# A two-stage adapter kernel: generator and first down-projections one step later, tile 1 in its own PSUM banks, other orders at both ends

## The reference

```python
scale = cond @ norm_w.T + 1.0                                   # [32, 256]
h = x * (scale[:, None, :] * rsqrt(mean(x * x) + 1e-6))
val, gate = split(h @ up_w.T, 2)                                # 1024 each
h = val * gelu(gate)
hq = round(h * 127 / max|h| per row) * max|h| / 127             # to 8 bits
wq = clip(round(down_w / mean|down_w|), -1, 1) * mean|down_w|   # ternary
x1 = hq @ wq.T + x

Wd_b = Wd + 0.1 * (cond @ Wdd.T + bdd)       # one 128 x 256 matrix for each sequence
Wu_b = Wu + 0.1 * (cond @ Wdu.T + bdu)       # one 256 x 128 matrix for each sequence
out = x1 + relu(x1 @ Wd_b.T + bd) @ Wu_b.T + bu
```

## Time and profile before

| | |
|---|---|
| median of 3 runs | 480.67 us (480.03 to 480.86) |
| the profiled execution | 480.89 us, its span 479.2 us |
| PE busy | 467.1 us, 97% |
| DVE, ACT, POOL busy | 377.8 (79%), 365.5 (76%), 260.2 us (54%) |
| mean granted TensorE clock | 0.995 of full speed |
| HBM read, written | 37.44 MB, 8.39 MB |

### The profile page before, as it was taken

The page is one execution under the profiler, slowest core; times in us unless marked ns, Lnnn a source line. Parts: engine busy times, 40 slices in busy tenths (PEclk is TensorE's granted clock), DMA queues, the critical chain, the costliest instruction groups (busy, mean ns, idle before and its releaser), DMA issues.

```text
span 479.2 us, 10039 instructions
## 1 busy us (share of the span) xinstructions
PE 467.1 (97%) x3278; PEld 271.3 (57%) x3278; DVE 377.8 (79%) x789; ACT 365.5 (76%) x636; POOL 260.2 (54%) x676
## 2 busy tenths in 40 slices
PE   8989999999999999999999999999999999999995
PEld 7445656666565455555555555555555555555563
DVE  4798988898898787877877788786777877777776
ACT  5889999999997678768676876867776777777662
POOL 0295775657655446475573746557374543444653
PEclk9999999999999999999999999999999999999997
DMA  7957787777873455565554466455445544544332
GB/s 269 349 113 205 180 244 227 189 210 181 253 176 89 92 121 100 137 147 117 148 133 107 128 141 155 111 153 126 103 136 133 143 103 119 130 123 90 72 85 89
DMA packets 117860, 71.01 MB, mean 148 GB/s; under 512 B 102000, under 2 KB 102960, under 8 KB 115632
## 3 DMA queue, kind: packets, MB, share of 16 engines
q1 hardware_dynamic: 117648, 70.29, 57.2%
q10 hardware_dynamic: 160, 0.07, 0.1%
HBM read 37.44 MB, written 8.39 MB: 96 GB/s over the span
## 4 chain that ended last, share of the span: by engine, by line
PE 88%; DVE 5%; ACT 3%; issue 2%; DMA 1%; POOL 0%; DVEq 0%; ACTq 0%; SPq 0%; POOLq 0%
PE bank L1022 64%; PE bank L1036 11%; PE bank L1113 4%; PE bank L1127 4%; PE bank L1095 4%; PE bank L993 1%; DVE adapt L716 1%; ACT gel L552 1%; DVE xs_lo L746 1%; DMA qT<-qn 1%; DVE hid L767 1%; DVE amax L775 1%; ACT tern L650 0%; ACT qn L574 0%; DVE x L879 0%
## 5 line engine op out<-in xcount | busy, mean ns | idle before, releaser
L767 DVE SCALAR_TENSOR_TENSOR hid<-bank,rms,gel 128x512 f32<-128x512 f32 x127 | 95.2, 750 | 80.4 <-ACT gel L552 79.4
L552 ACT ACTIVATE gel<-bank,rms 128x512 f32<-128x512 f32 x127 | 86.9, 684 | 90.7 <-PE bank L1022 90.6
L1022 PE MATMUL bank<-up_hi,xs_hi 128*128 128x512 f16 x508 | 151.2, 379 | 3.0 <-DVE hid L767 1.5
L1022 PE MATMUL bank<-up_lo,xs_hi 128*128 128x512 f16 x508 | 151.1, 379 | 0.7 <-DVE up_lo L931 0.7
L1022 PE MATMUL bank<-up_hi,xs_lo 128*128 128x512 f16 x508 | 151.1, 379 | 0.0
L1022 PEld LDWEIGHTS bank<-up_lo,xs_hi 128*128 128x128 f16 x508 | 49.6, 98 | 60.9 <-DVE up_lo L931 1.4
L1022 PEld LDWEIGHTS bank<-up_hi,xs_lo 128*128 128x128 f16 x508 | 49.7, 98 | 59.9
L775 DVE TENSOR_REDUCE amax<-hid 128x1 f32<-128x1024 f32 x63 | 76.9, 1220 | 2.2
L565 ACT ACTIVATE hid<-hid,amax 128x1024 f32<-128x1024 f32 x64 | 72.4, 1132 | 2.3 <-DVE amax L781 1.8
L403 POOL TENSOR_TENSOR wsplit<-stage,wsplit 128x288 f16<-128x288 f32 x64 | 52.8, 853 | 34.9 <-ACT wsplit L527 34.9
L1022 PEld LDWEIGHTS bank<-up_hi,xs_hi 128*128 128x128 f16 x508 | 48.3, 98 | 38.5 <-DVE xs_lo L746 2.9
(11 more groups left out here) (129 smaller groups left out, 633.3 us busy)
## 6 DMA issues: line engine op xcount, KB each, us to landing
xT_s<-in_xT SPq DMA_DIRECT2D x32, 256.0 KB, 3.0
xn_s<-in_xn SPq DMA_DIRECT2D x32, 256.0 KB, 3.1
stage<-in_WddT SPq DMA_DIRECT2D x8, 1024.0 KB, 5.4
stage<-in_WduT SPq DMA_DIRECT2D x8, 1024.0 KB, 5.2
out<-out_s SPq DMA_DIRECT2D x31, 256.0 KB, 2.4
adapt<-in_up_wT SPq DMA_DIRECT2D x4, 512.0 KB, 6.8
x<-in_down_wT SPq DMA_DIRECT2D x1, 1024.0 KB, 10.0
qT<-qn SPq DMA_TRANSPOSE x63, 3.1
```

Source lines behind the costliest of these rows:

```text
L552: nc.scalar.activation(gel[:, c], u_gate[c][:], ACT.Gelu, scale=rms[:, t // TPB % XN_SLOTS, t % TPB:t % TPB + 1]).then_inc(gelu_done, 1)
L767: nc.vector.scalar_tensor_tensor(out=hid[:, t % 2, c * 512:(c + 1) * 512], in0=u_val[c][:], scalar=rms[:, t // TPB % XN_SLOTS, t % TPB:t % ...
L1022: ins = nc.tensor.matmul(dst[:], a[:, t // TPB % 2, k, cols], w[:, c, k, v, :], start=(k == 0 and n == 0), stop=(k == KD - 1 and n == 2))
```

## The change

Generator chunks move one step later (`chunk`), and with them the adapter (`adapter_step`). The root of sequence 2 is at step 3. Down-projections 0 and 1 are both in step 4, and down(2) in step 5 as before; residual(0) is in step 4, residual(1) and (2) in step 5. Tile 1's up-projection goes to banks 5, 6, 7 and 4 and waits for nobody. The absolute sum is made in two halves, as the down weights come in two, and PE adds the two in bank 5 in step 2; ternary_first moves from step 1 to step 2, ternary_second ahead of, and ternary_third behind, quant_scale(2). The first root and the squares of sequences 0 and 1 go behind the up weights' conversion, xn of sequences 0 and 1 behind the up weights in the queue, base and bias ahead of sequence 2 and chunk 0. Two `idle` matmuls go. In the tail q_transpose goes ahead of down(62), middle(30) ahead of the last transposes, output_bias(30) ahead of middle_low(29), total(28) and residual_high(61) ahead of the evacuation of the transposed tile.

```diff
-N_SMALL = 6
+N_BASE = 4
+N_SMALL = 2
-IDLE_SECOND = 9
+IDLE_SECOND = 7
...
 def adapter_step(b):
-    return max(2 * b + 7, NGEN + 5 + (4 * b + 2) // 3)
+    return max(2 * b + 7, NGEN + 6 + (4 * b + 2) // 3)
 def scales(s):
-    return [b for b in range(1, B) if max(2 * b - 2, 1) == s]
+    return [b for b in range(2, B) if max(2 * b - 2, 3) == s]
+def downs(s, c):
+    late = {(4, 0): [0], (4, 1): [1]}
+    return late.get((s, c), [s - DOWN] if c == 0 and s - DOWN >= 2 else [])
+def residuals(s):
+    return {4: [0], 5: [1, 2]}.get(s, [s - DOWN] if s - DOWN > 2 else [])
 def chunk(s, lag):
-    return [s - 2 - lag] if 0 <= s - 2 - lag < NGEN else []
+    return [s - 3 - lag] if 0 <= s - 3 - lag < NGEN else []
...
-        sum_ps = y_ps[:, 0:1]
+        sum_ps = bank[5][:, 0:1]
+        second_val = [bank[5], bank[7]]
+        second_gate = [bank[6], bank[4]]
+        def u_banks(t, c):
+            return (second_val[c], second_gate[c]) if t == 1 else (u_val[c], u_gate[c])
...
@@ SP, before the loop
-            load_x(0)
+            sp.dma_start(xT_s[:, 0], xT[0]).then_inc(ld_xT[0], 16)
             for n in range(NC * KD):
                 sp.dma_start(raw_up[:, n // KD, n % KD], up_wT[:, n // KD, n % KD]).then_inc(ld_up[n], 16)
-            load_x(1)
-            sp.dma_start(raw_down, down_wT).then_inc(ld_down, 16)
+            for b in range(2):
+                sp.dma_start(xn_s[:, b], xn[b]).then_inc(ld_xn[b], 16)
+            for i in range(2):
+                part = slice(i * JF * D // 2, (i + 1) * JF * D // 2)
+                sp.dma_start(raw_down[:, part], down_wT[:, part]).then_inc(ld_down[i], 16)
+                if i == 0:
+                    sp.dma_start(xT_s[:, 1], xT[1]).then_inc(ld_xT[1], 16)
+            for i, (w, b) in enumerate(((WdT, bddT), (WuT, bduT))):
+                sp.dma_start(base[:, i, :], w).then_inc(ld_base, 16)
+                sp.dma_start(bias_raw[:, i, :], b).then_inc(ld_base, 16)
+            load_x(2)
             load_chunk(0)
-            load_x(2)
...
@@ POOL
             def base_sum():
-                pool.wait_ge(ld_small, 16 * N_SMALL)
+                pool.wait_ge(ld_base, 16 * N_BASE)
...
             residual_low(LAST_T - 2)
+            output_bias(B - 2)
             middle_low(B - 3)
-            output_bias(B - 2)
+            pool.wait_ge(x1_lo_done, LAST_T - 2)
+            output_bias_last(1)
             middle_low(B - 2)
-            output_bias_last()
+            output_bias_last(0)
@@ ACT
+            def absolute_sum(i):
+                part = slice(i * JF * D // 2, (i + 1) * JF * D // 2)
+                act.wait_ge(ld_down[i], 16)
+                nc.scalar.activation(tern[:].rearrange("p j d -> p (j d)")[:, part], raw_down[:, part], ACT.Abs,
+                                     accum_out=wsum[:, 3 * i:3 * i + 1]).then_inc(absum_ready, 1)
             scaled_high(0)
-            squares(0)
             (the four up_hi)
+            squares(0)
+            squares(1)
+            absolute_sum(0)
             for s in range(NT):
...
                 gelu(s, 0)
                 if s == 0:
+                    gelu(0, 1)
                     scaled_high(1)
-                    squares(1)
-                    gelu(0, 1)
-                    (the absolute sum)
+                if s == 1:
+                    absolute_sum(1)
+                    gelu(1, 1)
...
             quantized(LAST_T)
+            residual_high(LAST_T - 2)
             qT_evacuate()
-            residual_high(LAST_T - 2)
@@ DVE
             scaled_low(0)
-            rsqrt_guess(0)
-            rsqrt_first()
             (the four up_lo)
+            rsqrt_guess(0)
+            rsqrt_first()
+            rsqrt_guess(1)
             for s in range(NT):
...
                 gate(s, 0)
-                if s == 0:
-                    scaled_low(1)
-                    rsqrt_guess(1)
                 if s == 2:
-                    ternary_second()
-                    ternary_third()
-                if s >= DOWN:
-                    residual(s - DOWN)
+                    ternary_first()
+                for t in residuals(s):
+                    residual(t)
...
                     gate(s, 1)
+                    if s == 0:
+                        scaled_low(1)
+                    if s == 2:
+                        ternary_second()
                     quant_scale(s)
-                    if s == 1:
-                        ternary_first()
+                    if s == 2:
+                        ternary_third()
...
             residual(LAST_T - 2)
+            total(B - 4)
             qT_evacuate()
...
-            total(B - 4)
@@ PE
             def up(t, c):
-                after(pe, gelu_done, (t - 1) * NC + c + 1)
-                after(pe, hid_done, (t - 1) * NC + c + 1)
+                held = 0 if t == 2 else t - 1
+                if t != 1:
+                    after(pe, gelu_done, held * NC + c + 1)
+                    after(pe, hid_done, held * NC + c + 1)
...
                 up(s, 0)
-                if s >= DOWN:
-                    down(s - DOWN)
+                if s == 2:
+                    pe.wait_ge(hid_done, NC + 1)
+                    pe.wait_ge(absum_ready, 2)
+                    nc.tensor.matmul(sum_ps, ones[:], wsum[:, 0:1], start=True, stop=False)
+                    nc.tensor.matmul(sum_ps, ones[:], wsum[:, 3:4], start=False, stop=True).then_inc(absum_full, 1)
+                for t in downs(s, 0):
+                    down(t)
                 (up(s, 1), or the two pieces of tile 63)
-                if s == 1:
-                    (the sum, one matmul)
+                for t in downs(s, 1):
+                    down(t)
...
+            q_transpose()
             down(LAST_T - 1)
-            q_transpose()
             down_last()
...
             x_transpose(LAST_T, x63_hi_ps, (0,))
+            middle(B - 2)
...
             output(B - 3)
-            middle(B - 2)
```

More of the change, by code:

```diff
@@ L211, in build @@
         ld_cond = sem("ld_cond")
+        ld_base = sem("ld_base")
         ld_small = sem("ld_small")
@@ L214, in build @@
         ld_up = [sem(f"ld_up{i}") for i in range(NC * KD)]
-        ld_down = sem("ld_down")
+        ld_down = [sem(f"ld_down{i}") for i in range(2)]
         ld_xT = [sem(f"ld_xT{i}") for i in range(XT_SLOTS)]
@@ L453, in residual_low, with output_bias_last @@
                                         ).then_inc(late_lo_done, 1)
[L455 to L459, removed]
+            def output_bias_last(i):
+                pool.wait_ge(x1_done, LAST_T + i)
+                nc.gpsimd.tensor_tensor(late_out[:, i], x1[:, (LAST_T - 1 + i) % X1_SLOTS], bu_row[:], ALU.add
+                                        ).then_inc(outb_done, 1)
             def output_bias(b):
@@ L496, in _ @@
                 for b in scales(s):
-                    if b > 1:
-                        rsqrt(b)
+                    rsqrt(b)
                 if s == LAST_T - 1:
@@ L551, in gelu @@
                 act.wait_ge(u_full, t * NC + c + 1)
-                nc.scalar.activation(gel[:, c], u_gate[c][:], ACT.Gelu,
+                nc.scalar.activation(gel[:, c], u_banks(t, c)[1][:], ACT.Gelu,
                                      scale=rms[:, t // TPB % XN_SLOTS, t % TPB:t % TPB + 1]).then_inc(gelu_done, 1)
@@ L645, in _ @@
                 if s == 0:
+                    gelu(0, 1)
                     scaled_high(1)
-                    squares(1)
-                    gelu(0, 1)
-                    act.wait_ge(ld_down, 16)
-                    nc.scalar.activation(tern[:].rearrange("p j d -> p (j d)"), raw_down, ACT.Abs,
-                                         accum_out=wsum[:, 0:1]).then_inc(absum_ready, 1)
+                if s == 1:
+                    absolute_sum(1)
+                    gelu(1, 1)
                 if s >= 1:
@@ L660, in _ @@
                     quantized(s - 1)
-                if 0 < s < LAST_T:
+                if 1 < s < LAST_T:
                     gelu(s, 1)
@@ L667, in _ @@
                 for b in scales(s + 1):
-                    if b > 1:
-                        squares(b)
+                    squares(b)
             gelu_piece(1)
@@ L767, in gate @@
                 nc.vector.scalar_tensor_tensor(
-                    out=hid[:, t % 2, c * 512:(c + 1) * 512], in0=u_val[c][:],
+                    out=hid[:, t % 2, c * 512:(c + 1) * 512], in0=u_banks(t, c)[0][:],
                     scalar=rms[:, t // TPB % XN_SLOTS, t % TPB:t % TPB + 1], in1=gel[:, c],
@@ L954, in _ @@
                 for b in scales(s):
-                    if b > 1:
-                        rsqrt_guess(b)
+                    rsqrt_guess(b)
                 for b in adapter_splits(s):
@@ L1020, in up @@
                             pe.wait_ge(up_ready, c * KD + k + 1)
-                        for v, dst in enumerate((u_val[c], u_gate[c])):
+                        for v, dst in enumerate(u_banks(t, c)):
```

(5 more changed lines are left out.)

3 lines of the change are left out of this document (removed).

## The result

The changed kernel takes **484.27 us** (median of 5 runs, 483.98 to 484.98); the kernel before, run beside it, 480.67 (480.03 to 482.0). The ratio is 1.0075, 95% interval 1.0060 to 1.0089: slower by 3.6 us, as forecast (483.7, 479.6 to 486.9). The profiled execution took 483.98 us, span 482.3 against 479.2.

The account below looks back on a forecast made before the run. PE (TensorE) was taken to bound the kernel, holding 88% of the chain. 480.9 + 5.8 (front) + 0.8 (clock) - 1.0 (step 20) - 2.6 (tail) = 483.9, so 483.7 us on the runs' scale; range 479.6 to 486.9.

Parts of the forecast that it names:

- step 20: Last evacuations move from step 19 to 20, so PE's 1.09 us wait at 157.27 goes: -1.0, bounds -1.1 and 0.
- the first wait: PE at down(1) waits 4.8 us for residual(0), which hangs on POOL's root of sequence 2 behind chunk 0.
- the second: PE at down(2) waits 2.0 us by order alone, as DVE runs residual(1) behind gate(5, 0).
- rival (b): Faster: root of sequence 2 ready by 37, PE never waits at down(1), 478.1 us; chance 0.16.
- The front, 5.8: Front end up to up(6, 0) loses 5.8 us, gain at the start included; bounds 4.8 to 7.1.
- the start: Up weights land sooner, PE ends up(0, 1) near 14.5, some 1.4 us sooner; bounds 1.0 and 1.6.
- base sooner: Base moved ahead of sequence 2 and chunk 0 in the queue: counted at nothing.
- The root: Root of sequence 2 on POOL taken as 3.2 us, not 4.2, since no ternary pass runs beside it.
- The clock, 0.8: Half clock on PE in the stretch behind 44.0: 0.8 us more, bounds 0 and 1.7.
- The tail, -2.6: Behind the loop: -2.6 us if the slow clock also leaves the last matmuls, -1.3 without; at most -3.5.
- POOL's order: In the tail, output_bias no longer beside the two residual_low, so they take 0.85 for 1.69: -0.8.
- the pair of q_transpose and the sooner passes: In the tail, q_transpose fills the wait for the last transposing DMA and down_last ends 0.4 sooner.

Follow-up runs that it names:

- experiment 1: Changed kernel, but in step 3 POOL makes the root of sequence 2 ahead of the low part of generator chunk 0: 477.66 us, ratio to before 0.9935.
- experiment 2: Changed kernel with one number of scales() put back, so the root of sequence 2 is at step 2: 479.07 us, ratio to before 0.9973.
- experiment 3: Changed kernel, but DVE makes residual(1) in step 4, right behind gate(4, 1): 481.85 us, ratio to before 1.0024.
- experiment 9: Kernel before with only generator chunks a step later and adapter_step's NGEN + 6 for NGEN + 5: 480.32 us, ratio to before 0.9999.
- experiment 4: Changed kernel with idle(11), 22 passes of useless matmuls, on PE ahead of down(1) in step 4: 482.92 us, ratio to before 1.0041.
- experiment 5: Changed kernel with idle(22), useless matmuls on PE, in the wait ahead of down(1): 483.26 us, ratio to before 1.0045.
- experiment 10: Changed kernel with the root of sequence 2 ahead of low_part(0) on POOL and residual(1) behind gate(4, 1): 474.96 us, ratio to before 0.9870.
- experiment 6: Kernel before with all the change's edits behind the loop and none ahead: 477.58 us, ratio to before 0.9942.

## Why the prediction was right, and where two of its terms were not

**What held.** The mechanism: POOL runs the chunk ahead of the root of sequence 2, down(1) waits for what hangs on it (at 43.56; forecast 44.0, after a wait of 5.3; forecast 4.8), down(2) waits by the order alone (2.11; forecast 2.0), and step 20's wait goes. Experiments 1 and 2 (the first wait), 3 (the second) and 9 (step 20) show each by taking it away. The faster rival (b) needed a root by 37; it was done at 41.5.

**The front, 5.8: measured 5.3.** Up(6, 0) starts at 57.90, 6.25 after before's 51.65; less 2.4 of clock, plus 1.4 for the owed chunk: 5.3. Two links were shorter than I took them. Up(0, 1) ended at 14.05 and not 14.5 (the last up weight landed near 11.1, not 11.55), so the start won 1.9 and not 1.4. That is partly this execution's luck: with the same start up(1, 0) began between 13.97 and 14.90 in the traces of experiments 1 to 5 and 10. And ternary_second took 1.22 us and not 1.63, since base_sum had left POOL by then. The DVE timeline of the changed kernel, then POOL's:

```profile
24.15 1.30 DVE L761 TENSOR_SCALAR x<-x,wsum 128x2048 f32<-128x2048 f32 x1
...
26.71 1.22 DVE L766 TENSOR_SCALAR x<-x 128x2048 f32<-128x2048 f32 x1
...
29.36 1.21 DVE L771 TENSOR_SCALAR tern<-x 128x2048 bf16<-128x2048 f32 x1
```

```profile
21.51 1.28 POOL L497 TENSOR_TENSOR base<-base,bias_raw 128x512 f32<-128x512 f32 x1
22.88 1.49 POOL L499 TENSOR_SCALAR base<-base 128x512 f32<-128x512 f32 x1
```

In before these two POOL passes lay beside DVE's ternary passes and took 2.12 and 3.01:

```profile
25.26 2.12 POOL L474 TENSOR_TENSOR base<-base,bias_raw 128x512 f32<-128x512 f32 x1
27.47 3.01 POOL L476 TENSOR_SCALAR base<-base 128x512 f32<-128x512 f32 x1
```

So "base sooner" was not worth nothing, as I had it: the prediction's own row of 1.63 was a contended one. The Trainium skill (SBUF — State Buffer, "Who interferes with whom") says that GpSimd and a two-port VectorE instruction exclude each other; the pair 3.01 and 1.49 for one pass agrees. The root took 3.2 (38.32 to 41.52) as I chose, beside an idle DVE. The reason that I gave for it was wrong all the same: no ternary pass ran beside before's root of 4.2. Its multiply of 1.06 (from 33.62) lay beside DVE's low part of the chunk (33.55 to 34.62). Beside ternary passes the root is seen in experiment 2, where two of its instructions took 1.05 and 1.20 (at 27.85 and 30.35) against 0.20 and the whole root 5.1.

**The clock, 0.8: measured 2.4.** This term was mis-sized, by a factor of three. I took the length of the tail's slow spell, 3.4 us, as the most and about half of its cost. This spell lasted 6.8 us, of which 5.0 lay over work (43.56 to 48.6). Experiment 1's trace gives 2.35 for it and experiment 4's profiled execution, at an equal start of down(1), 2.36. The sentence that failed is the bound "up to 3.4 us of work cost up to 1.7 more": it rested on one spell, in another place, behind shorter waits.

**The tail, -2.6: measured -3.6** by the ruler and -3.1 in experiment 6. I had split it into a version in which the slow clock leaves the last matmuls and one in which it doesn't, and the first came true. That it did is not shown to be the edits' work: in experiment 9 the clock held in before's own tail. At equal clock the orders are worth 3.1 (17.56 - 14.50). The split over edits was partly wrong: POOL's order gives about 0.4 on the path where I wrote 0.8, and the pair of q_transpose and the sooner passes 1.4 where I wrote 0.4. The recorded terms also don't carry their own bounds: without the clock's part they add up to 1.9 (0.4, 0.8 and 0.7) and not to 1.3, and nothing stands behind the 3.5.

**Step 20, -1.0:** right at its place (experiment 9), and there it is seen that the move costs about as much in the front end of before. In the prediction this cost was part of the 5.8.

Together: 5.3 + 2.4 - 1.0 - 3.6 = 3.1 against 5.8 + 0.8 - 1.0 - 2.6 = 3.0. The direction and the waits were foreseen; that the total was met to 0.1 us of the span (0.6 us in the medians) is luck, since the errors of clock, tail and front cancel (+1.6, -1.0, -0.5).

## What to carry to other kernels

Where a step of work is moved, list on each engine what it now stands ahead of: here four passes moved ahead of a small root cost 5 us of waiting, and exchanging the two turned a loss of 3.6 us into a gain of 3.0. A wait of several microseconds on TensorE costs more than its length, since the clock may fall behind it (here 2.4 us on top of 5.3): price it with the clock's rows. And an edit that wins nothing in total (the generator a step later) can hide a gain of 1.1 us and a loss as large, which only a ruler along the span shows.

## What the runs showed of the hardware that I had not expected

- In these traces the granted clock fell behind some short waits and not behind others of about the same length: behind 2.33 us in experiment 2 and 2.11 in experiment 5, not behind 2.02 and 2.11 in experiment 1, nor behind 2.79 in experiment 4. Each kernel has one trace, but the mean clocks of its other runs differ in the same steps. The 1 us of scatter of the kernel before goes with them: 479.77 and 480.77, as above; the four runs of experiment 10 are all at 0.999 or 1.0 and lie within 0.9 us.
- Slow spells over work came in two lengths in these traces: 3.4 us (before from 470.5, experiment 2 from 33.6, experiment 5 from 51.3, experiment 6 from 11.2) and 6.8 (the changed kernel from 41.8, experiment 3 from 42.4).
- The same 128x128 float32 passes took 0.24 us each at the start of experiment 5 (16 in 3.78 us) and 0.115 in its fill (44 in 5.07). The windows give 1.00 as granted clock for both. But the first pair of up-projection matmuls behind the start's passes took 1.06 there, as pairs did at a granted 0.50 in experiment 2 (34.10), and 0.59 from 10.6 on:

```profile
9.12 1.06 PE L1055 MATMUL bank<-up_hi,xs_hi 128*128 128x512 f16 x2
```

So the durations at the start are those of the lower level. Why the clock's row doesn't show it stays open.
